# Loading the adjacency from GpSimd's queue with a cast to bytes, and packing products put singly behind the others

## The reference

```python
# layer 0: graph attention, residual, layer norm
Wh = x @ W                                   # 128 -> 128
e  = (Wh @ a1)[:, None] + (Wh @ a2)[None, :]
e  = where(e > 0, e, 0.2 * e)
e  = where(adj > 0, e, -9e15)
x  = layernorm(x + elu(softmax(e, axis=1) @ Wh))
# layer 1: mean over neighbours, linear, residual, layer norm
x1 = adj.astype(float32) @ x / adj.sum(axis=1, keepdims=True)
x  = layernorm(x + concatenate([x1, x], axis=1) @ weight + bias)
```

## Time and profile before

| | |
|---|---|
| median of 3 runs | 1607.88 us (1607.56 to 1608.36) |
| profiled execution, its own time | 1608.12 us |
| its span, first to last instruction | 1606.30 us |
| granted TensorE clock, mean | 0.988 |
| adjacency loads | 128 of 2048 KB |

### The profile page before, as it was taken

One profiled execution on the slowest core, in us unless ns is written; L12 is line 12 of the kernel. 1 busy time (PEld: TensorE's weight loads), 2 busy tenths in 40 slices (PEclk: granted clock), 3 DMA queues, 4 the chain that ended last, 5 costly groups with the idle time before them and its releaser, 6 DMA issues. The chain is left out here.

```text
span 1606.3 us, 46438 instructions
## 1 busy us (share of the span) xinstructions
PE 1557.2 (97%) x16966; PEld 1372.1 (85%) x16966; DVE 871.3 (54%) x3335; ACT 1002.7 (62%) x2513; POOL 437.4 (27%) x571
## 2 busy tenths in 40 slices
PE   7599999999999999999999999999999999999998
PEld 6488888888888888888888888887888888888886
DVE  7965555555555555555555555554444445454443
ACT  3999899989998999899988998881100000010000
POOL 0033443344334433443344334430000000000000
PEclk9799999999999999999999999999999999999999
DMA  8668777777777777777777777742000000000000
GB/s 272 237 258 280 274 274 283 278 274 274 280 280 276 274 276 275 285 274 274 280 282 271 273 286 278 270 136 64 20 16 16 16 16 16 16 19 17 16 16 16
DMA packets 100733, 302.84 MB, mean 189 GB/s; under 512 B 5729, under 2 KB 67937, under 8 KB 67937
## 3 DMA queue, kind: packets, MB, share of 16 engines
q1 hardware_dynamic: 100704, 302.48, 52.9%
HBM read 289.77 MB, written 12.68 MB: 188 GB/s over the span
## 5 line engine op out<-in xcount | busy, mean ns | idle before, releaser
L476 ACT ACTIVATE level_ring<-s_row,cols 128x256 fp8e4<-128x256 f32 x2048 | 839.3, 498 | 0.0
L684 PE MATMUL acc<-factors,edge_ring 128*128 128x258 f16 x4096 | 541.7, 273 | 17.7 <-issue 11.9
L684 PE MATMUL acc<-factors,level_ring 128*128 128x258 f16 x4096 | 541.1, 273 | 0.0
L746 PE MATMUL acc<-factors,adj_ring 128*128 128x258 f16 x4096 | 471.1, 274 | 3.6 <-DMA factors<-x_parts 3.0
L684 PEld LDWEIGHTS acc<-factors,edge_ring 128*128 128x128 fp8e4 x4096 | 390.8, 98 | 75.8 <-issue 20.0
L746 PEld LDWEIGHTS acc<-factors,adj_ring 128*128 128x128 fp8e4 x4096 | 400.5, 98 | 63.2 <-DMA factors<-x_parts 3.3
L684 PEld LDWEIGHTS acc<-factors,level_ring 128*128 128x128 fp8e4 x4096 | 399.6, 98 | 59.4
L919 DVE TENSOR_TENSOR level_ring<-level_ring,edge_ring 128x1024 uint16<-128x1024 uint16 x256 | 176.8, 692 | 237.7 <-ACT level_ring L476 226.8
L584 ACT ACTIVATE part_sums<-acc 128x258 f32<-128x258 f32 x32 | 12.4, 386 | 295.2 <-PE acc L746 295.2
L926 DVE TENSOR_TENSOR edge_ring<-edge_ring,level_ring 128x1024 uint16<-128x1024 uint16 x256 | 181.3, 739 | 0.0
L358 POOL TENSOR_SCALAR one<-mv 128x2 f32<-128x2 f32 x64 | 24.7, 387 | 549.4 <-DVE mv L971 549.4
(11 more groups left out here) (101 smaller groups left out, 840.4 us busy)
## 6 DMA issues: line engine op xcount, KB each, us to landing
adj_ring<-in_adj SPq DMA_DIRECT2D x128, 2048.0 KB, 7.7
x_parts<-parts SPq DMA_DIRECT2D x32, 129.0 KB, 4.8
factors<-x_parts SPq DMA_DIRECT2D x8, 516.0 KB, 3.9
factors<-in_x SPq DMA_DIRECT2D x8, 512.0 KB, 7.2
s_row<-s_and_t SPq DMA_DIRECT2D x32, 128.0 KB, 4.5
rows_x<-in_x SPq DMA_DIRECT2D x32, 128.0 KB, 4.5
x_rows<-rows_y SPq DMA_DIRECT2D x32, 128.0 KB, 7.9
rows_x<-x_rows SPq DMA_DIRECT2D x32, 128.0 KB, 2.1
```

Of the source, the lines that this page charges most:

```text
L476: a = act.activation(level_bytes[:, h % MASK_SLOTS, j, :, :], s_halves[:, slot, :, :], ACT.Relu, bias=t_big[:, h * HALF + j:h * HALF + j + ...
L684: m = pe.matmul(acc[a][:, 0:ROW], mask, factors[:, neg, jj, :], start=(jj == 0), stop=(jj == NJ - 1))
L746: m = pe.matmul(acc[b][:, 0:ROW], ring_1_bytes[:, c, j, b, :], factors[:, 0, jj, :], start=(jj == 0), stop=(jj == NJ - 1))
```

## The change

Four things. (1) The 128 loads of the adjacency leave SyncE's queue and are issued by GpSimd. (2) They cast int32 to uint8 on the way, so that a chunk takes 4 KB per partition and not 16, and there are four slots, one for each c; the packing products read adjacent bytes. `packed` starts at 0, and the load of (g, c) waits for the packing of (g-1, c). (3) The four loads of group 0 are issued at the start, behind the landing of part of x; those of groups 1 and 2 ahead of `output_0(0)`; those of group g+3 within `output_0(g)`, one behind each of its four parts. (4) In a half-chunk with a packing to do, each of the 32 long products is followed by one packing product, where a block of 32 followed the half-chunk; `acc_done` and `mask_used` are raised by the same long products as before.

```diff
-ADJ_SLOTS = 2
+ADJ_SLOTS = 4
...
-        adj_ring = sb("adj_ring", [P, ADJ_SLOTS, TPG, COLS], I32)
+        adj_space = sb("adj_space", [P, N], I32)
...
+        adj_ring = adj_space[:, :].bitcast(U8)[:, 0:ADJ_SLOTS * TPG * COLS]\
+            .rearrange("p (s t c) -> p s t c", s=ADJ_SLOTS, t=TPG)
...
-        adj_in = [sem("adj_in0"), sem("adj_in1")]
+        adj_in = [sem(f"adj_in{c}") for c in range(ADJ_SLOTS)]
...
@ sync
-            def load_adj(g, c):
-
-                sp.wait_ge(packed, UPG * g + c + 1)
-                sp.dma_start(adj_ring[:, c % ADJ_SLOTS, :, :], adj_tiles[g, :, :, c * COLS:(c + 1) * COLS])\
-                    .then_inc(adj_in[c % ADJ_SLOTS], 16)
-            sp.sem_inc(packed, ADJ_SLOTS)
...
@ gpsimd
+            def load_adj(g, c, first=False):
+
+                if not first:
+                    pool.wait_ge(packed, UPG * (g - 1) + c + 1)
+                    pool.sem_inc(adj_free, 1)
+                pool.dma_start(adj_ring[:, c, :, :], adj_tiles[g, :, :, c * COLS:(c + 1) * COLS]).then_inc(adj_in[c], 16)
+
             pool.memset(minus_half, -0.5).then_inc(half_ok, 1)
+            pool.wait_ge(x_in_sem[NX // 2 - 3], 16)
+            for c in range(UPG):
+                load_adj(0, c, first=True)
...
-            def output_0(g, first=False):
+            def output_0(g, first=False, loads=True):
                 softmax_rows(g)
+                if loads:
+                    load_adj(g + 3, 0)
                 elu_and_residual(g, first)
+                if loads:
+                    load_adj(g + 3, 1)
                 scale_and_shift(g)
+                if loads:
+                    load_adj(g + 3, 2)
                 low_parts(g)
+                if loads:
+                    load_adj(g + 3, 3)
+
+            for g in (1, 2):
+                for c in range(UPG):
+                    load_adj(g, c)
             pool.wait_ge(one_row_ok, 1)
             output_0(0, first=True)
-            with pool.Fori(1, NG - 1) as g:
+            with pool.Fori(1, NG - 3) as g:
                 output_0(g)
+            with pool.Fori(NG - 3, NG - 1) as g:
+                output_0(g, loads=False)
...
@ tensor
+            def pack_tile(c, i):
+
+                j, t = i // TPG, i % TPG
+                low_bytes = adj_ring[:, c, t, j * P:(j + 1) * P].bitcast(F8)
+                words_t = pack_ps[c % 2][:, j * WPG:(j + 1) * WPG].rearrange("p (w t) -> p w t", t=TPG)[:, :, t]
+                return pe.matmul(words_t, low_bytes, pack_w[:, :], start=True, stop=True)
...
@ tensor, multiply: inside the loop over j
-                    if h == 7 and a < 2 * TPG - 1:
-                        m.then_inc(acc_done, 1)
-                m.then_inc(mask_used, 1)
+                        if h == 7 and a < 2 * TPG - 1 and j == HALF - 1:
+                            m.then_inc(acc_done, 1)
+                        if a == 2 * TPG - 1 and j == HALF - 1:
+                            m.then_inc(mask_used, 1)
+                        if pack_chunk is not None:
+                            w = pack_tile(pack_chunk, a * HALF + j)
+                if pack_chunk is not None:
+                    w.then_inc(packed, 1)
...
@ tensor, group
-                        multiply(g, h, first and h % 2 == 0, first)
-                    if not last:
-                        pack(c)
+                        multiply(g, h, first and h % 2 == 0, first, c if h % 2 and not last else None)
```

More of the change, by code:

```diff
@@ L29 @@
 U16 = mybir.dt.uint16
+U8 = mybir.dt.uint8
 I32 = mybir.dt.int32
@@ L132, in adj_resnorm_kernel @@
         wq, w_turn, a_sb, s_turn, sum_xb = (early_of[n] for n in ("wq", "w_turn", "a_sb", "s_turn", "sum_xb"))
-        ring_1 = adj_ring[:, :, :, :].rearrange("p s t c -> p (s t c)").bitcast(U16)[:, 0:RING_1 * UNIT * P]\
+        adj_ring = adj_space[:, :].bitcast(U8)[:, 0:ADJ_SLOTS * TPG * COLS]\
+            .rearrange("p (s t c) -> p s t c", s=ADJ_SLOTS, t=TPG)
+        ring_1 = adj_space[:, :].bitcast(U16)[:, ADJ_SLOTS * COLS:ADJ_SLOTS * COLS + RING_1 * UNIT * P]\
             .rearrange("p (s j r) -> p s j r", s=RING_1, j=UNIT)
@@ L166, in adj_resnorm_kernel @@
         score_ok, mask_ok, mask_used, acc_done, neg_ready = (sem(n) for n in "score_ok mask_ok mask_used acc_done neg_ready".split())
-        slot_free, masks_there, sums_read = (sem(n) for n in "slot_free masks_there sums_read".split())
+        slot_free, masks_there, sums_read, adj_free = (sem(n) for n in "slot_free masks_there sums_read adj_free".split())
         pos_copied, neg_added, nd_ok, flag_ok, full_ok, inv_den_ok, hidden_ok, exp_in_ok, exp_ok, elu_ok = (
@@ L201, in adj_resnorm_kernel @@
         wh_all = wide_f32[:, N:N + NJ * F].rearrange("p (j f) -> p j f", f=F)
-        adj_all = adj_ring[:, :, :, :].rearrange("p s t c -> p (s t c)")
+        adj_all = adj_space[:, :]
         adj_01 = adj_all.bitcast(F32)
@@ L259, in _ @@
             load_s(1, 1)
-            load_adj(0, 3)
             load_x(0, True)
@@ L267, in _, with group @@
             sp.sem_inc(wh_saved, 1)
[L269 to L273, removed]
+            def group(g, slot, first=False, s_next=True):
                 if not first:
@@ L450, in copy_words @@
             def copy_words(g, c):
-                act.wait_ge(packed, UPG * g + c + 1 + ADJ_SLOTS)
+                act.wait_ge(packed, UPG * g + c + 1)
                 act.activation(words[:, g, c * WPU:(c + 1) * WPU], pack_ps[c % 2][:, 0:WPU], ACT.Copy)\
@@ L635, in packable @@
             def packable(g, c, first=False):
-                pe.wait_ge(adj_in[c % ADJ_SLOTS], 16 * (UPG // ADJ_SLOTS * g + c // ADJ_SLOTS + 1))
+                pe.wait_ge(adj_in[c], 16 * (g + 1))
                 if not first:
                     pe.wait_ge(words_ok, UPG * g + c - 1)
-            def pack(c):
-                for j in range(UNIT):
-                    for t in range(TPG):
-                        low_bytes = adj_ring[:, c % ADJ_SLOTS, t, j * P:(j + 1) * P].bitcast(F8)\
-                            .rearrange("p (c b) -> p c b", b=4)[:, :, 0]
-                        words_t = pack_ps[c % 2][:, j * WPG:(j + 1) * WPG].rearrange("p (w t) -> p w t", t=TPG)[:, :, t]
-                        m = pe.matmul(words_t, low_bytes, pack_w[:, :], start=True, stop=True)
+            def pack_tile(c, i):
[3 more added lines that the diff above has]
+                return pe.matmul(words_t, low_bytes, pack_w[:, :], start=True, stop=True)
+            def pack(c):
+                for i in range(UNIT * TPG):
+                    m = pack_tile(c, i)
                 m.then_inc(packed, 1)
@@ L667, in _, with multiply @@
                 pack(c)
-            def multiply(g, h, factors_in=False, first=False):
+            def multiply(g, h, factors_in=False, first=False, pack_chunk=None):
                 pe.wait_ge(mask_ok, 8 * g + h + 1)
```

3 lines of the change are left out of this document (removed).

## The result

| | before | after |
|---|---|---|
| median | 1607.72 us (1606.16 to 1608.36, 4 runs) | 1684.3 us (1682.93 to 1685.76, 4 runs) |
| span of the profiled execution | 1606.3 us | 1682.2 us |
| granted TensorE clock, mean | 0.988 | 0.984 |

The changed kernel takes 1.0478 times as long (95% interval 1.046 to 1.0496): 76.6 us more, where 106 were forecast and 1605 to 1800 us given as range. The place and the kind of the wait are the forecast ones. Four of its terms are off, and the total is as near as it is because they offset each other in part. Two made the forecast too high, a clock loss that came in one group only (23 us forecast) and `scale_and_shift` (21 us). One made it too low, the start (13 to 15 us, forecast at nothing). The fourth, that single packing gains nothing, is wrong by itself but made no difference here.

A forecast was written before the change was run, and what follows sets the result against it. The prediction took TensorE to bound layer 0, 32.21 us a group, with ScalarE having only 2.38 us to spare. 29 group edges x (2.85 + 0.8) = 106 us on 1608.1 gave 1714 us, range 1605 to 1800.

The forecast's parts named there:

- The wait: On GpSimd, load 1 ahead of scale_and_shift waits for chunk 1's packing; TensorE stalls 1.43 us + X per group.
- X: GpSimd's time to issue a load, taken as 1.42 us from its longest pass over 128 partitions x 2 rows.
- `scale_and_shift`: GpSimd's step ahead of ScalarE's normalise: begins 3.76 us + X later, its 2.53 us to normalising kept as before.
- The clock: TensorE idle 3.1 us at each group's edge, slowing its clock in half of the groups: 0.8 us a group.
- The start: Before layer 0, new first loads change nothing, as the first long product waits for VectorE, full from 40 to 80 us.
- The cast: In the adjacency loads, casting adds nothing; it would bind only from 1.43 times as long as plain loads.
- Rival 2: In the adjacency loads, the cast halves the DMA rate: 520 us more, about 2130 us; chance 0.15.
- Packing singly: On TensorE, each packing product behind a long one costs 25 ns as in the block: nothing gained.
- rival 4: On TensorE, packing products hide wholly under long ones: 1644 us, or 1692 us with the clock lost; chance 0.11.
- 1: On GpSimd, a load's issue waits for VectorE's unpacking runs, stall 4.3 us a group: 1780 us; chance 0.13.
- 3: On GpSimd, the wait does not hold its arithmetic and packing costs as before: no change, 1608 us; chance 0.04.
- 5: On TensorE, alternating hides weight loads and a load costs GpSimd next to nothing: faster, 1594 us; chance 0.06.

The follow-up runs named there:

- Experiment 1: Changed kernel with the four loads of output_0(g) rotated one place later, so the load ahead of scale_and_shift has its chunk long packed: 1616.2 us, ratio 1.0043.
- e5: Changed kernel with three loads behind scale_and_shift, one behind low_parts, and a two-element GpSimd addition ahead of the start's loads: 1591.5 us, ratio 0.9885.
- e8: Kernel before, each group's first product also waiting for GpSimd's fill step of the group before, idle pieces of 3.16 us: 1763.0 us, ratio 1.097.
- e9: Kernel before, each group's first product also waiting for GpSimd's step after the fill step, idle pieces of 3.98 us: 1775.5 us, ratio 1.1038.
- experiment 2: Changed kernel with one two-element addition on GpSimd behind partition_all_reduce, ahead of the loads of groups 1 and 2: 1671.8 us, ratio 1.0391.
- e6: Changed kernel with packing products again in one block of 32 per chunk, loads and cast still on GpSimd: 1686.0 us, ratio 1.0478.

## Why the prediction was right, and where it was off

**The wait.** Right in place, mechanism and releaser: load 1 stands ahead of `scale_and_shift` on GpSimd and can't be issued before chunk 1 is packed, and normalising, copy and the next group move with it. Experiment 1 took that wait away and 58 us of period with it. In us after TensorE's start of the group:

| | forecast | measured |
|---|---|---|
| packing of chunk 1 done, and 0.17 | 16.22 | 16.13 (last product from 538.15 to 538.32, + 0.17, less 522.36) |
| load, to the start of `scale_and_shift` (X) | 1.42 | 1.41 |
| `scale_and_shift` to normalising | 2.53 | 1.82 |
| normalising to the next group | 14.89 | 15.00 |
| period | 35.06 | 34.36 |

**X.** Right in size, by a lucky neighbour. The load itself is 0.74 us; the rest lies between the last packing product and the load, 0.76 instead of SyncE's 0.17, and 0.08 behind it. GpSimd also raises a semaphore (`adj_free`) in those 0.76 us, which SyncE did not; what it takes of them was not tried. Neither part has to do with a pass over 128 x 256 elements, the row it was taken from.

**`scale_and_shift`.** The failed size of the stall. I moved its 2.53 us as they were in the earlier trace rows. Moved, its first and last instruction take 0.25 and 0.20 us, not 0.56 and 0.51; 0.71 us a group are saved, 29 x 0.71 = 21 us. In e5, where it stands at its old place among VectorE's work, it has its old durations (the last one 0.50 us). What of VectorE's work makes the difference was not tried.

**The clock.** This term was wrong, 23 us forecast for 1.5 in one group. The mechanism was real: e8 and e9 show it at about the size that I gave. The step that failed was the one before it, that all idle time stands at the group's edge in one piece of 3.1 us. I followed the delay from the normalising only to the copy of the sums. It also runs over the scores and the last negative mask to the positive mask of h = 6, and there it stops TensorE some 9 us earlier. The same lateness was paid in two pieces, and where it came in one, at 1029.39, the clock was lost. The Trainium skill (TensorE: Matmul & The Clock Gate, HAM oscillation) describes a kernel in which a pause in each round costs the clock in each round. e9's groups agree, 1.6 us each; e8's do but for four of 31; the changed kernel's two short pieces are no such pause.

**The start.** Forecast at nothing, measured at 15.2 us to the first softmax step; some 2 us of it came back by the end. I looked for what TensorE waits for and stopped at VectorE. Two things were missed: eight loads with waits now stand between `partition_all_reduce` and GpSimd's first arithmetic, so that its pause of 10 us no longer lies in 60.7 us of idle time, and the loads' early issue delays `s_row`. Both show in experiment 2, which gave back 12.5 us. The idle time ahead of GpSimd's first softmax step was in the trace of before, put down to VectorE; that a pause was hidden in it could not be read there.

**The sum.** Forecast 29 x (1.43 + 1.42 + 0.8) = 106. Measured 29 x (1.43 + 1.41 - 0.71) = 62, and 13 to 15 at the start: 76. Without the clock's term the forecast would have been 83, near the truth by two errors, +21 and -15. With it, it was 30 us too high, and that it came no further off is luck: the missed start hid a third of the other two errors.

**The cast.** Nothing, as taken: 25.1 us of DMA time a group against 24.5, and the landing (least, median and most us of the 128 loads) against the earlier trace rows:

```profile
DMA to landing us min/median/max: 7.6/7.8/21.8
```

Rival 2 is out. e5 says it in time as well: same period with cast loads as without.

**Packing singly.** 25 ns each was right (24), and rival 4, that they hide under the long ones, is out. That it gains nothing was wrong by itself: the 0.41 us of the loop's edge went, and I had counted them as TensorE's fixed share without asking what stands ahead of the edge. In the changed kernel the error cost nothing, as e6 shows, because the loop over GpSimd set the period.

**The other rivals.** 1, that a load's issue waits for VectorE's runs: no load took over 1.1 us (least, median and most ns of the 128 loads were 713, 793 and 1093), and the 0.75 us ahead of a load are the same at load 3 (555.38 to 556.12), where VectorE is idle all through them. The Trainium skill (SBUF — State Buffer, Who interferes with whom) warns of this; here the spread of 0.38 us bounds what it did to an issue. 3 is out. 5, the faster kernel, needed packing products that hide, and they don't. That the change can gain all the same, 17 us with the loads behind `scale_and_shift`, comes from the loop's edge, which no rival had.

## What to carry to other kernels

When a DMA issue with a wait moves onto an engine that computes, write down for each instruction behind it who waits for it, and put the wait behind the last one on the critical path: here one place was worth 58 us, and no load ahead of `scale_and_shift` with a start put right made a loss of 77 us a gain of 17, the whole of what single packing gives by itself. Follow a delay on every branch and not on the first one that reaches the bounding engine, since where idle time falls decides whether it costs clock too. And before counting a saving, ask whether the engine that saves still sets the period.

## What the runs showed of the hardware

- GpSimd's first ordinary arithmetic behind `partition_all_reduce` came after a pause of 7.6 us (e2) and 10.1 us (the changed kernel), once in each.
- A load issued by GpSimd held it for 0.74 us with 256 rows of 8 KB and for about 0.57 with 128; it started 0.76 us behind the last product that it waited for, with one more semaphore to raise, where SyncE's issue started 0.17 us behind.
- A cast from int32 to uint8 on the way hardly changed the DMA engines' time (25.1 us a group for 24.5) or the median landing (7.8 us for 7.7).
- The edge of TensorE's loop cost 0.41 us behind a block of 32 short products and nothing visible behind alternating ones.
- Equal idle pieces of 3.16 us at TensorE cost from nothing (four of 31) to 2.5 us more by the clock; two of 1.07 and 1.34 us in a group cost nothing, and one of 2.43 (e6) or 2.77 us (the changed kernel) cost 1.5 us.
